# Attention and channel mixing in one kernel: every group two query tiles, two key blocks a step, two banks of sums and five work banks

## The reference

```python
x = y_all                                     # (2, 2048, 256)
n = layernorm(x)
q = (n @ Wq + bq) / 16;  k = n @ Wk + bk;  v = n @ Wv + bv
w = softmax(where(causal, q @ k.T, -inf))
x = x + (w @ v) @ Wo + bo
n = layernorm(x);  prev = n shifted by one row (zero first)
xr = mu_r*n + (1-mu_r)*prev;  xk = mu_k*n + (1-mu_k)*prev
out = x + sigmoid(xr @ W_r) * (relu(xk @ W_k)**2 @ W_v)
```

## Time and profile before

| | us |
|---|---|
| time, median of 3 runs | 389.09 (388.43 to 390.05) |
| the profiled execution's own time | 390.67 |
| its span, first to last instruction | 388.9 |
| TensorE busy | 357.9 |
| VectorE busy | 260.7 |
| ScalarE busy | 244.5 |
| GpSimd busy | 210.0 |

### The profile page before, as it was taken

The page is one execution under the profiler, slowest core; times in us unless marked ns, Lnnn a source line. Parts: engine busy times, 40 slices in busy tenths (PEclk is TensorE's granted clock), DMA queues, the critical chain, the costliest instruction groups (busy, mean ns, idle before and its releaser), DMA issues.

```text
span 388.9 us, 6803 instructions
## 1 busy us (share of the span) xinstructions
PE 357.9 (92%) x2433; PEld 322.3 (83%) x2433; DVE 260.7 (67%) x596; ACT 244.5 (63%) x496; POOL 210.0 (54%) x250
## 2 busy tenths in 40 slices
PE   3798999989899999899999799998999989999885
PEld 3576788979799788789998689987889979999874
DVE  3559596598656796945279678487864477576655
ACT  1134636776587476598533974873768658777973
POOL 1111333456368751869732385742575479589861
PEclk9899999999999999999999999999999999999999
DMA  7600000000002000200030000200000000000101
GB/s 200 205 0 3 0 2 0 3 1 3 27 2 81 2 1 29 82 2 0 2 110 1 2 0 28 83 0 2 1 2 29 1 29 1 29 27 17 41 1 54
DMA packets 11891, 10.66 MB, mean 27 GB/s; under 512 B 1873, under 2 KB 11858, under 8 KB 11858
## 3 DMA queue, kind: packets, MB, share of 16 engines
q1 hardware_dynamic: 11858, 10.23, 8.5%
HBM read 6.04 MB, written 4.19 MB: 26 GB/s over the span
## 4 chain that ended last, share of the span: by engine, by line
PE 49%; DVE 19%; ACT 12%; POOL 10%; issue 7%; DMA 2%; SPq 0%; ACTq 0%; DVEq 0%
PE W L683 10%; PE W L686 10%; PE W L687 10%; PE O L830 5%; PE O L832 5%; PE O L831 5%; DVE mix L601 5%; POOL p_lo L304 3%; DVE peak L557 3%; ACT st L381 2%; DVE xhat L488 2%; ACT mix L399 2%; POOL mix_lo L315 2%; DMA x_in<-in_L_attn_y_all_dram 2%; ACT st L345 1%
## 5 line engine op out<-in xcount | busy, mean ns | idle before, releaser
L304 POOL TENSOR_TENSOR p_lo<-st,p_hi 128x512 fp32r<-128x512 f32 (+1 forms) x94 | 91.7, 995 | 49.1 <-ACT p_hi L345 48.0
L557 DVE TENSOR_TENSOR peak<-peak,W 128x512 f32<-128x512 f32 (+3 forms) x85 | 44.7, 526 | 78.4 <-ACT st L345 76.8
L830 PE MATMUL O<-v_hi,p_hi 128*128 128x258 f32 x272 | 78.8, 290 | 4.3 <-POOL p_lo L304 4.2
L832 PE MATMUL O<-v_hi,p_lo 128*128 128x258 f32 x272 | 76.7, 282 | 0.0
L831 PE MATMUL O<-v_lo,p_hi 128*128 128x256 f32 x272 | 76.4, 281 | 0.0
L683 PE MATMUL W<-xT_hi,kT_hi 128*128 128x512 f32 (+2 forms) x188 | 65.9, 351 | 7.8 <-DVE peak L557 4.3
L381 ACT ACTIVATE st<-st 128x512 f32<-128x512 f32 (+1 forms) x94 | 47.3, 504 | 37.5 <-DVE st L569 37.5
L345 ACT ACTIVATE st<-W 128x512 f32<-128x512 f32 (+1 forms) x94 | 44.3, 475 | 35.9 <-PE W L687 35.5
L686 PE MATMUL W<-xT_lo,kT_hi 128*128 128x512 f32 (+2 forms) x188 | 65.8, 350 | 0.0
L687 PE MATMUL W<-xT_hi,kT_lo 128*128 128x512 f32 (+2 forms) x188 | 63.2, 336 | 0.0
L830 PEld LDWEIGHTS O<-v_hi,p_hi 128*128 128x128 f32 x272 | 51.2, 188 | 6.5 <-POOL p_lo L304 5.9
(11 more groups left out here) (112 smaller groups left out, 764.4 us busy)
## 6 DMA issues: line engine op xcount, KB each, us to landing
x_in<-in_L_attn_y_all_dram SPq DMA_DIRECT2D x8, 512.0 KB, 5.0
out_dram<-gate SPq DMA_DIRECT2D x15, 256.0 KB, 2.1
h_row<-in_L_attn_Wk_dram SPq DMA_DIRECT2D x1, 256.0 KB, 2.8
h_row<-in_L_attn_Wq_dram SPq DMA_DIRECT2D x1, 256.0 KB, 3.2
st<-in_L_attn_Wv_dram SPq DMA_DIRECT2D x1, 256.0 KB, 6.1
st<-in_L_attn_Wo_dram SPq DMA_DIRECT2D x1, 256.0 KB, 6.2
mix<-in_L_ffn_W_k_dram SPq DMA_DIRECT2D x1, 256.0 KB, 4.1
mix<-in_L_ffn_W_r_dram SPq DMA_DIRECT2D x1, 256.0 KB, 4.4
```

The costliest lines, as they stand in the source:

```text
L304: g.tensor_tensor(p_lo[:, u % NP, r], score_tile(u), p_hi[:, u % NP, r].bitcast(f32), ALU.subtract)\
L557: v.tensor_tensor(peak[:, J % 2, r], peak[:, J % 2, r], scores, ALU.max).then_inc(maxed, 1)
L830: mm(bank_o[q][:, 0:VW], p_hi[:, u % NP, w], v_hi[:, j, :], start=j == 0, stop=False)
L832: last = mm(bank_o[q][:, 0:VW], p_lo[:, u % NP, w], v_hi[:, j, :], start=False, stop=end)
```

## The change

All groups are of two query tiles (16 groups), and a step takes two key blocks: the left half of a work bank holds block j against the two tiles, the right half block j+1. That is 72 steps, each 512 columns wide with twelve products of 256 columns. On the diagonal a block that lies above it is masked whole, with a mask of 256 columns. The units of the second half of the kernel (`PARTS`) stay as the groups were before. A group's maxima are gathered and spread over both halves of the bank. PSUM is cut anew: two sum banks O used in turn, five work banks W, bank B. A new group's first `pv` waits until the tile two before has left its sum bank (`o_used`). Shifts get slots of their own (`SUB_AT`): four of a group a slot from the spread on, or earlier with the exp. All tables are new, with 277 instead of 349 slots.

The beginning: the weights and x lead SyncE's queue, x of group 0 comes in four transfers with a semaphore each, group 1 of x before the second half's weights; the small vectors go through ScalarE's queue. Twenty-two products of zeros (`idle`) stand between the first pieces on TensorE. ScalarE takes over the query weights' part of `taken`, GpSimd puts in the bias columns. The first `kT` starts with its high-by-high products once the high halves of `xT` and `wkq` are there, and takes the low halves last; it uses two banks side by side. The second half's weights are transposed in slots -3, 1 and 2 (2, 3 and 11 before).

```diff
-    NW = 3
+    NW = 5
+    NO = 2
-    GROUPS = [(G, 0, TG) for G in range(NG - 1)] + [(NG - 1, 0, TG // 2), (NG - 1, TG // 2, TG // 2)]
+    GROUPS = [(G, t0, TG // 2) for G in range(NG) for t0 in (0, TG // 2)]
+    PARTS = [(G, 0, TG) for G in range(NG - 1)] + [(NG - 1, 0, TG // 2), (NG - 1, TG // 2, TG // 2)]
+    WIDE = [TG // n for G, t0, n in GROUPS]
+    COUNT = [(TG * (G % GB) + t0 + n) // (TG // n) for G, t0, n in GROUPS]
...
+    PV_AT = [9, 11, 15, 18, 18, 18, 20, 20, 24, 24, 26, 26, 26, 26, 26, 28, 29, 29, 30, 30, 30, 31, 31, 31, 35, 37, 37, 37, 38, 38, 39, 40, 40, 40, 40, 40, 44, 46, 46, 54, 54, 55, 56, 56, 57, 57, 59, 59, 62, 62, 63, 67, 67, 67, 70, 71, 75, 94, 94, 102, 104, 127, 128, 128, 133, 141, 141, 145, 151, 152, 166, 168]
+    MT_AT = [(1,), (6,), (10,), (13,), (18,), (25,), (29,), (36,), (38,), (40,), (46,), (50,), (55,), (58,), (65,), (114,)]
+    MB_AT = [(2,), (8,), (10,), (15,), (20,), (26,), (30,), (36,), (38,), (40,), (48,), (51,), (56,), (60,), (68,), (128,)]
+    KT_AT = {1: (3, 3), 2: (10, 10), 3: (16, 26), 4: (33, 34), 5: (40, 40), 6: (45, 47), 7: (58, 58)}
+    FT_AT = [(-3,), (1,), (2,)]
+    IDLE = (6, 1, 5, 6, 4)
...
+    SUB_AT = [min(P_AT[u], MB_AT[STEPS[u][0]][0] + 1 + (u - FIRST[STEPS[u][0]]) // 4) for u in range(NS)]
...
     # loads
-                for i, vec in ((BK, bk), (BQ, bq)):
-                    sp.dma_start(cols[:, i, :], vec.rearrange("(k p) -> p k", p=P)).then_inc(qk_loaded, 16)
             sp.dma_start(raw_k, halves(wk)).then_inc(wk_loaded, 16)
             sp.dma_start(raw_q, halves(wq)).then_inc(wq_loaded, 16)
-            load(0)
+            for t in range(TG):
+                sp.dma_start(x_in[:, 0, t, :], y_t[:, t, :]).then_inc(x0_loaded[t], 16)
             sp.dma_start(raw_v, halves(wv)).then_inc(wv_loaded, 16)
             sp.dma_start(raw_o, halves(wo)).then_inc(wo_loaded, 16)
+            load(1)
...
+            sc.wait_ge(fold_ready, 2)
+            high(minus_first[:], pairs(early[1])[:, :, 0], minus_ready, scale=-1.0)
+            sc.wait_ge(minus_ready, 1)
+            for d in range(KC):
+                last = a.activation(wqT[:, d, 1:C], early[1][:, d * C + 1:(d + 1) * C], ACT.Identity, bias=minus_first[:, d:d + 1])
...
     # scores
+                for b in range(WIDE[J]):
+                    r = cols_of(s) if WIDE[J] == 1 else slice(b * n * P, (b + 1) * n * P)
+                    left = min(r.start, r.stop - 2 * P)
+                    stop = (t0 + n) * P
+                    q = slice(stop - (r.stop - left), stop)
+                    keys, mask = slice((j + b) * P, (j + b + 1) * P), None
+                    if diagonal(s, b) >= t0:
+                        at = r.start + (0 if WIDE[J] == 1 else (diagonal(s, b) - t0) * P)
+                        m0 = P if WIDE[J] == 1 or b == 0 else 0
+                        mask = (bank[:, at + m0 - P:at + P], ident_b[:], mask_b[:, m0:])
+                    last = product(bank[:, left:r.stop],
+                                   [(kT_hi[:, k, keys], kT_lo[:, k, keys], xT_hi[:, G % NT, k, q], xT_lo[:, G % NT, k, q])
+                                    for k in range(KC)], mask)
+                last.then_inc(s_ready, 1)
...
     # pv
+                for b in range(WIDE[J]):
+                    for q in tiles_of(u, b):
+                        tile, o = G * TG + q, o_of(G, q)
+                        if j + b == 0 and tile >= NO:
+                            pe.wait_ge(o_used, tile - NO + 1)
...
+            def idle(n):
+                for _ in range(n):
+                    mm(early[3][:], warm[:, 0:P], warm, start=True, stop=True)
...
+            for w, x, wait in ((wkq_hi, xh, None), (wkq_lo, xh, (fold_split, 1)), (wkq_hi, xl, (xT_split, KC))):
+                if wait:
+                    pe.wait_ge(*wait)
+                for h in range(KC):
+                    for k in range(KC):
+                        last = mm(bank_of("kT", 0, h)[:], w[:, k, h * P:(h + 1) * P], x[:, k, :], start=x is xh and w is wkq_hi and k == 0,
+                                  stop=x is xl and k == KC - 1)
```

More of the change, by code:

```diff
@@ L76, in attention_channel_mix_block, with span, pair, last_group @@
     FILLED = {n: s for s, (n, _) in enumerate(PLACES)}
-    def span(J):
-        G, t0, n = GROUPS[J]
+    def span(K):
+        G, t0, n = PARTS[K]
         return slice(t0 * P, (t0 + n) * P)
-    def pair(J, i):
-        return (GROUPS[J][0] * TG + GROUPS[J][1]) // 2 + i
+    def pair(K, i):
+        return (PARTS[K][0] * TG + PARTS[K][1]) // 2 + i
+    def last_group(G):
+        return max(J for J in range(NJ) if GROUPS[J][0] == G)
     def block_steps(G, chunk):
-        J = max(J for J in range(NJ) if GROUPS[J][0] == G)
-        return FIRST[J] + TG * (chunk + 1)
+        J = last_group(G)
+        return FIRST[J] + TG * (chunk + 1) // WIDE[J]
@@ L91, in attention_channel_mix_block, with part_of @@
+    def part_of(G, p):
+        return next(K for K, (B_, t0, n) in enumerate(PARTS) if B_ == G and t0 <= p < t0 + n)
     FIRST_SLOT = -3
     WARM = (4, 3)
[L93 removed]
@@ L326, in _ @@
                     weights_low(u)
-                for u in DONE_IN.get(s - 1, ()):
-                    rsqrt2(u)
+                for u, p in DONE_IN.get(s - 1, ()):
+                    rsqrt2(u, p)
                 for stage, n, i in STAGES.get(s - 1, ()):
@@ L438, in _ @@
             sc.wait_ge(fold_ready, 5)
-            high(wvo_hi[:], pairs(bank_o[0]), fold_moved)
+            high(wvo_hi[:], pairs(early[0]), fold_moved)
             for s in SLOTS:
@@ L538, in _ @@
             v.memset(hT[:, :, 0:1], 0.0).then_inc(prev_ready, 1)
-            for h in range(KC):
-                kT_part(0, h)
-            dve.wait_ge(fold_moved, 2)
-            low(wvo_lo[:], bank_o[0][:].rearrange("p (k c) -> p k c", k=KC), wvo_hi[:], fold_split)
             def take_max(s):
@@ L638, in _ @@
             for s in SLOTS:
-                for u in P_IN[s]:
+                for u in SUB_IN[s]:
                     shift(u)
@@ L642, in _ @@
                     take_max(s)
-                for u in DONE_IN.get(s - 2, ()):
-                    h_part(u)
-                for u in DONE_IN.get(s - 1, ()):
-                    x1_part(u)
+                for u, p in DONE_IN.get(s - 2, ()):
+                    h_part(u, p)
+                for u, p in DONE_IN.get(s - 1, ()):
+                    x1_part(u, p)
                 for stage, n, i in STAGES[s]:
@@ L783, in scores @@
                 G, t0, n = GROUPS[J]
-                r = cols_of(s)
-                left = min(r.start, r.stop - 2 * P)
-                q = slice(t0 * P + left, t0 * P + r.stop)
-                keys = slice(j * P, (j + 1) * P)
+                bank = bank_of("S", s, 0)
                 free("S", s, 0)
@@ L792, in scores @@
                     pe.wait_ge(kT_split, KC * (G + 1))
-                bank, mask = bank_of("S", s, 0), None
-                if diagonal(s) >= t0:
-                    mask = (bank[:, r.start:r.start + P], ident_b[:], mask_b[:])
-                product(bank[:, left:r.stop],
-                        [(kT_hi[:, k, keys], kT_lo[:, k, keys], xT_hi[:, G % NT, k, q], xT_lo[:, G % NT, k, q])
-                         for k in range(KC)], mask).then_inc(s_ready, 1)
+                for b in range(WIDE[J]):
[12 more added lines that the diff above has]
+                last.then_inc(s_ready, 1)
             def gather_peak(J):
-                n = GROUPS[J][2]
+                n, w = GROUPS[J][2], WIDE[J]
                 if J > 0:
@@ L873, in _ @@
                 for d in range(KC):
-                    last = mm(bank_o[0][:, h * C:(h + 1) * C], wvT[:, d, h * P:(h + 1) * P], raw_o[:, d, :],
+                    last = mm(early[0][:, h * C:(h + 1) * C], wvT[:, d, h * P:(h + 1) * P], raw_o[:, d, :],
                               start=d == 0, stop=h > 0 and d == KC - 1)
                 if h == 0:
-                    mm(bank_o[0][:, 0:C], ident[0:1, :], bo_row, start=False, stop=True)
+                    mm(early[0][:, 0:C], ident[0:1, :], bo_row, start=False, stop=True)
             last.then_inc(fold_ready, 1)
```

231 lines of the change are left out of this document (129 added, 102 removed).

## The result

The changed kernel takes 375.89 us (median of 4 runs, 375.76 to 376.08) against 389.57 for the kernel before on the same chip: the ratio is 0.9624, 95% interval 0.9587 to 0.966. That is 3.8% or some 14 us faster. The forecast of 382.5 had the direction right and half of the size; 375.9 lies near the lower bound of its range, 374. The profiled execution has a span of 374.1 us against 388.9.

The account below looks back on a forecast made before the run. TensorE, busy 92%, was taken as the bound, standing still 33.8 us; 388.9 - 5 (beginning) + 11.9 (work) - 13.7 (stalls) = 382.1 for the span, stated as 382.5 us for the median, range 374 to 393, the forecast's own 378 to 387.

Parts of the forecast that it names:

- Beginning: Stretch before the first score product: it would start at about 18 instead of 22.98 us, -5 us, bounds -2.5 to -7.
- The 22 zero products: Waits of TensorE before the first score: fill them, full clock from there on, at no cost; 4.7 us if half ran late.
- Work: TensorE's products over the whole kernel: 4.1 us more for scores, 7.0 for transposes, 0.8 for masks, +11.9, bounds +9 to +15.
- the wider masks: Score products on the diagonal: half the masks get 256 wide, +0.8 us on TensorE.
- The transposes: Gather and spread of the maxima on TensorE: 128 instead of 64 at 0.11 us each, +7.0 us.
- The rival by the busy share of weight loads: TensorE's weight loads: they bind, with 65 us more of loads, for a time over 400 us; chance 0.03.
- Stalls: TensorE's waits behind the first score: 13.7 of 33.8 us go, leaving 20; bounds of what goes 7 to 24.
- Rival 1: TensorE's waits in the loop: the order is looser than credited, 22 to 24 us of stalls go, giving 374; chance 0.20.
- Early slots "as ragged as they are": First third of batch 0, VectorE's work nearly equal to TensorE's: no gain and no loss there, bounds -1 to +4 us.
- Two sum banks: Start of each group: first value products wait until both tiles before are normalised, 0 to 2 us, inside the remaining 20.
- Rival 3: Group boundaries: sum banks and VectorE's queue run late, six of 15 wait 2 us each, 12 us back, 394; chance 0.13.
- Shifts ahead: VectorE's shifts issued before the exp: cost VectorE nothing in sum, only take ScalarE's waits for it.

## Why the prediction was half the size

**Beginning, forecast -5, measured -3.9.** The chain moved as said: x's transposes at 11.16 (11.3 to 11.8), key products at 13.46 (12.8 to 13.5). Behind them I had 4.5 us to the first score and it took 5.7, since the second folded matrix, its bias and the moved transposes lie there one behind the other. The 22 zero products were counted as what brings the full clock; the run without them says that the gapless order does. I also read the clock of the kernel before as half up to 19 us; the row from 13 to 16 us above has 0.99, so it had risen and fell again behind the pause.

**Work, forecast +11.9, counted +10.7.** Four transposes moved ahead of the first score (0.4), and the wider masks (0.8) cost nothing. The transposes are paid nearly in full: doubling the 128 cost 13.4 to 14.1 us of 14.1. The rival by the busy share of weight loads (the Trainium skill's Perfetto Trace Analysis, Identifying the Most-Contended Engine) did not come: the share rose from 83% to 93%, and a product of 256 columns with its own load still starts every 0.119 us. As a measure of how full TensorE is the share does well here: the work by the count is 85% and 91% of the span.

**Stalls, forecast -13.7, counted -21.7. This is the step that failed.** I sized what the five banks free at the waits whose releaser was a maximum or a gated sum, 7.0 us, and put the rest to chains, to VectorE's load and to "many pieces under 0.25 us that no distance explains". The runs show in its place: the fourth bank alone is worth 22.3 us in the new order, the fifth 2. Waits named for `kT_lo`, `v_lo` and `xT_lo` come and go with the banks too, and so do the short pauses. In the kernel before they were seven waits of 4.2 us, 5.4 with the 0.17 us each that busy time hides; the forecast left them standing, and after the change all are gone. They are some two thirds of the eight missed; most of the rest is in pauses under 0.2 us. How much of the old order's 33.8 us were waits for banks stays open: four sum banks leave no room for a fourth work bank there, and two work banks were not run. That there are waits of the same names before and with three banks is the sign, not the proof. Rival 1 (374, chance 0.20) was the case that came; its argument, that distances are at two to four times the chain, is half of it. The new order keeps its distances with three banks and gains nothing from them; I read that as scores that need the banks to run ahead of the rest.

**Early slots "as ragged as they are".** Wrong: from 19.13 to 40 us TensorE has no idle time, with VectorE busy 17.9 of 20.9 us. Up to 60 us the stalls by the count are 0.9 us, against 4.8 before and 5.9 with three work banks. A full VectorE did not stop TensorE as long as there were banks between them.

**Two sum banks.** Forecast 0 to 2 us, measured nothing; TensorE's two waits are 0.9 us. Rival 3 did not come. **Shifts ahead** cost and gave nothing alone, as said. In the code a gather waits for all shifts of the group before (`sub_done`), so the early gathers of the new order need them; what they are worth there was not tried apart.

## What to carry to other kernels

Count TensorE's work by start-to-start distances and take it from the span: what is left are stalls, and that number, not the idle column, is what a change of order can win. Read a wait for an engine that reads a PSUM bank as a wait for the bank before reading it as one for the data, and price one bank more by all waits of that kind; here the fourth bank (22.3 us) paid for the extra work of the new order (10.7 us) twice over. Once TensorE is gapless, take work off it only where no other engine gets more.

## What the runs showed of the hardware

VectorE's normalisation of one tile (128x256, one input) takes 381 ns at the least, 407 in the median and 1394 at the most in the changed kernel:

```profile
L532 DVE TENSOR_SCALAR xhat<-x_in,mean_var,rstd x32: 381/407/1394, 9.6 to 254.5; 128x256 f32<-128x256 f32 x32
```

Three of the 32 take over a microsecond (1394, 1366 and 1384 ns, at 168.91, 189.97 and 253.15). Each begins while a GpSimd subtraction runs and ends 0.15 us behind that one's end; the second of them and its neighbour:

```profile
189.90 1.28 POOL L325 TENSOR_TENSOR p_lo<-st,p_hi 128x512 fp32r<-128x512 f32 x1
189.97 1.69 DVE L532 TENSOR_SCALAR xhat<-x_in,mean_var,rstd 128x256 f32<-128x256 f32 x2 [0.31 <-POOL rstd L313]
```

Where the normalisation began first, as at 252.83, it took 407 ns and the subtraction that began 0.13 us later 1430 instead of some 1290. The Trainium skill (SBUF — State Buffer, Who interferes with whom) says that such an operation can take a port pair that VectorE shares with GpSimd, and that the one who comes second is blocked for the whole of the other's instruction. The trace agrees, in both orders. No run tried it apart. The slow pair of 2.35 us at 169.73 in the kernel with half the transposes lies in the same way beside a `mix_lo` and two `p_lo`.

Of TensorE's clock: behind pauses of 2.0 to 2.8 us it is granted at 0.50, in the changed kernel once (at its last wait, worth 1.3 us), with three work banks three times more inside the loop, 1.5 us each. Not every such pause does it: the two of 2.1 and 2.8 us in the trace of the kernel with half the transposes did not.
